# A four-layer graph network on one core: the second layer's own-row work moved into its edge pass, and eight buffers of gathered rows in the third layer's

## The reference

```
out_gnn = relu(xn @ W1.T + segment_sum((xn @ W2.T)[src], dst))
q, k, v = split(xn @ w_qkv + b_qkv)          # 8 heads of 32 columns
k, v    = layernorm(k) * kln_g + kln_b, layernorm(v) * vln_g + vln_b
out     = q @ (k.T @ v / n)                  # per head
ret     = out + xn
h       = gelu(ret @ w1 + b1)
x       = x + out_gnn + (h @ w2 + b2 + xn)
```

## Time and profile before

| | us |
|---|---|
| median of 3 runs (9645.8 to 9689.9) | 9663.9 |
| profiled execution, its own time | 9673.6 |
| its span, first to last instruction | 9671.9 |
| PE busy | 5212.6 (54%) |
| VectorE busy | 5460.1 (56%) |
| ScalarE busy | 1976.8 (20%) |
| GpSimd busy | 3732.0 (39%) |

### The profile page before, as it was taken

How to read it: one execution, slowest core, us unless ns; L and a number is a source line. 1 busy time by engine, 2 the same in 40 slices (tenths; PEclk the granted TensorE clock), 3 DMA queues, 4 the chain that set the end, 5 groups by cost and what they waited for, 6 DMA issues and landing times. The chain is left out here.

```text
span 9671.9 us, 114565 instructions
## 1 busy us (share of the span) xinstructions
PE 5212.6 (54%) x21955; PEld 3844.8 (40%) x21956; DVE 5460.1 (56%) x12451; ACT 1976.8 (20%) x4673; POOL 3732.0 (39%) x3791
## 2 busy tenths in 40 slices
PE   3551454545565545644924454907666676665443
PEld 3551333333344523324813344803444434443243
DVE  5884555656663244464155554144888648885743
ACT  0000333133301100011212211201444124441111
POOL 0884566076501347500136620221655115550003
PEclk9999776767776866676967775958899788887767
DMA  1333333133304623301723311922666136661025
GB/s 56 127 127 41 98 105 99 31 104 101 88 6 140 209 77 88 75 7 59 279 58 84 82 34 51 305 57 90 183 185 186 40 105 183 181 183 47 5 72 168
DMA packets 585603, 1020.35 MB, mean 105 GB/s; under 512 B 187333, under 2 KB 352810, under 8 KB 576714
## 3 DMA queue, kind: packets, MB, share of 16 engines
q0 software_dynamic: 191616, 489.64, 19.4%
q1 hardware_dynamic: 363275, 496.15, 15.6%
q10 hardware_dynamic: 30528, 32.52, 1.0%
HBM read 927.10 MB, written 90.26 MB: 105 GB/s over the span
## 5 line engine op out<-in xcount | busy, mean ns | idle before, releaser
L663 POOL DMA_INDIRECT l_hgt_ep_g<-l_hgt_tkm,l_hgt_ep_ix x832 | 931.5, 1120 | 655.4 <-PE l_hgt_ep_out L739 446.3
L663 POOL DMA_INDIRECT l_gat_ep_g<-l_gat_th,l_gat_ep_ix x832 | 927.5, 1115 | 433.0 <-issue 234.0
L739 PE MATMUL l_hgt_ep_out<-l_hgt_ep_g,l_hgt_ep_here 128*126 128x288 f32 x1664 | 587.9, 508 | 511.4 <-DVE l_hgt_ep_g L874 311.1
L739 PE MATMUL l_gat_ep_out<-l_gat_ep_g,l_gat_ep_here 128*126 128x264 f32 x1664 | 626.5, 536 | 64.0 <-issue 30.0
L739 PEld LDWEIGHTS l_hgt_ep_out<-l_hgt_ep_g,l_hgt_ep_here 128*126 128x126 f32 x1664 | 364.8, 230 | 680.9 <-issue 577.8
L459 POOL DMA_INDIRECT recs<-place_stage,place_pos x400 | 520.4, 1301 | 288.7 <-issue 284.1
L663 POOL DMA_INDIRECT l_ep_g<-l_table,l_ep_ix x416 | 410.8, 987 | 233.6 <-issue 119.7
L1718 POOL IOTA f_moe_route_io<- 1x56 f32 (+2 forms) x4 | 0.7, 166 | 1289.8 <-ACTq L92 1289.8
L1907 DVE TENSOR_TENSOR f_moe_experts_yb<-f_moe_experts_py,f_moe_experts_b2s 128x256 f32<-128x256 f32 x208 | 88.4, 425 | 725.5 <-PE f_moe_experts_py L1890 694.1
L1055 PE MATMUL l_sum_out<-l_sum_g,l_sum_here 128*125 128x256 f32 x832 | 336.7, 540 | 290.4 <-DVE l_g L1080 121.9
L739 PEld LDWEIGHTS l_gat_ep_out<-l_gat_ep_g,l_gat_ep_here 128*126 128x126 f32 x1664 | 414.9, 264 | 188.2 <-issue 61.7
(11 more groups left out here) (575 smaller groups left out, 12169.7 us busy)
## 6 DMA issues: line engine op xcount, KB each, us to landing
l_hgt_ep_hot<-locrow SPq DMA_DIRECT2D x208, 256.0 KB
f_moe_experts_w1b<-in_L_ffn_w SPq DMA_DIRECT2D x32, 1024.0 KB
f_moe_experts_w2b<-in_L_ffn_w SPq DMA_DIRECT2D x32, 1024.0 KB
f_moe_experts_w1b<-in_L_ffn_w SPq DMA_DIRECT2D x64, 512.0 KB
f_moe_experts_w2b<-in_L_ffn_w SPq DMA_DIRECT2D x64, 512.0 KB
f_moe_experts_w1b<-in_L_ffn_W SPq DMA_DIRECT2D x56, 512.0 KB
f_moe_experts_w2b<-in_L_ffn_W SPq DMA_DIRECT2D x56, 512.0 KB
l_gat_ep_hot<-locrow SPq DMA_DIRECT2D x104, 256.0 KB
```

What stands on the lines that cost most here:

```text
L663: gp.indirect_dma_start(g[:, b % 4, j, 0:W], None, table, bass.IndirectOffsetOnAxis(ap=ix[:, b, j:j + 1].bitcast(U32), axis=0)).then_inc(s ...
L739: pe.matmul(out[:, t % 4, 0:WO], here[:, b % 2, t, :], g[:, b, t, F:F + WO], start=True, stop=True).then_inc(s_out, 1)
```

## The change

In the third layer, `edge_pass` of kind "ee" gets NB = 8 buffers of gathered rows, with a semaphore for each, instead of four; the loops of PE, ScalarE and VectorE are unrolled by eight there and GpSimd's by sixteen. The other kinds keep NB = 4.

In the second layer, `edge_sums` is gone and `layer1` is written out. A first phase (l1_pre) transposes each tile of xn once and keeps all 25, multiplies it with W2 and W1 side by side, stores the first as the table (VectorE copies it) and puts the second into the accumulator (ScalarE), in place of the memset. SP loads the weights of the whole layer ahead of the table's stores. VectorE then spreads the gains and takes the mean over each head's 32 columns off the k and v weights and bias, so that k and v come out of the projection with their means removed.

The second phase (l1_edges) is the pass over the edges, written out in straight-line code on PE, ScalarE and VectorE for all 104 chunks, with eight buffers for gathered rows. Between chunks 1 and 46 it projects one of the 25 tiles to k and v every 1.84 chunks, normalises it two and three chunks later, and adds its k.T v four chunks later. Around chunk 50 the mixer's matrix is formed, with the scale on it. From chunk 56 on it makes for each tile the mixer's output and ret, transposed, then the up product with gelu read out of PSUM, then the down product, added to x. x += xn is done per tile. After the last chunk one operation over all rows adds relu of the accumulator to x.

```diff
 def edge_pass(...):
+    NB = 8 if kind == "ee" else 4
-        ix = ph.sb("ix", [128, 8, CT], I32)
-        g = ph.sb("g", [128, 4, CT, max(F + WO, W)])
+        ix = ph.sb("ix", [128, 2 * NB, CT], I32)
+        g = ph.sb("g", [128, NB, CT, max(F + WO, W)])
-                if later(k, 4):
-                    gp.wait_ge(s_out, CT * (k - 3))
+                if later(k, NB):
+                    gp.wait_ge(s_out, CT * (k - NB + 1))
...
-def edge_sums(core, name, acc, table, idx):
...
 def layer1(core, x, xn):
-        edge_sums(core, "l1_sum", g, table, core.e_src)
-            project(core, "l1_self", xn, w, D, ("add", g))
...
+                            for k in range(2):
+                                mm = pe.matmul(out[:, t % 2, h, 0:D], xt[:, t, k, :], wp[:, k, D * h:D * h + D], start=k == 0, stop=k == 1)
...
+            RB = 8
+            SPAN = 46
+            kv_at = {1 + SPAN * t // NT: t for t in range(NT)}
+            out_at = {56 + SPAN * t // NT: t for t in range(NT)}
+            CHAIN = 2 + SPAN * (NT - 1) // NT + 4
...
+                def indices(i, b):
+                    if later(i, RB):
+                        gp.wait_ge(s_out, EG * (i - RB + 1))
+                    gp.tensor_copy(ix[:, b, :], core.e_src[:, bass.ds(i * EG, EG)]).then_inc(s_ix, 1)
...
+            def _(v):
+                edges_here(0)
+                for i in range(NG + 2):
+                    if i + 1 < NG:
+                        edges_here(i + 1)
+                    if 1 <= i <= NG:
+                        add(i - 1)
+                    if i - 1 in kv_at:
+                        t = kv_at[i - 1]
+                        v.wait_ge(s_kv, t + 1)
+                        if t >= 4:
+                            v.wait_ge(s_gram, t - 3)
+                        v.tensor_tensor(y[:, t % 4, :], side[0:P, 0, :], bkv[:, :], ALU.add).then_inc(s_y, 1)
+                        v.tensor_tensor(x[:, t, :], x[:, t, :], xn[:, t, :], ALU.add)
+                    if i - 2 in kv_at:
+                        t = kv_at[i - 2]
+                        v.wait_ge(s_sq, t + 1)
+                        v.tensor_reduce(ve[:, t % 4, :], sq[:, t % 2, :].rearrange("p (h c) -> p h c", c=32), AX.X, ALU.add)
+                        v.drain()
+                        v.tensor_scalar(ve[:, t % 4, :], ve[:, t % 4, :], 1.0 / 32, 1e-5, ALU.mult, ALU.add).then_inc(s_ve, 1)
+                    if i - 3 in kv_at:
+                        t = kv_at[i - 3]
+                        v.wait_ge(s_sd, t + 1)
+                        v.reciprocal(sd[:, t % 4, :], sd[:, t % 4, :])
+                        v.drain()
+                        y3 = y[:, t % 4, :].rearrange("p (h c) -> p h c", c=32)
+                        v.tensor_tensor(y3, y3, sd[:, t % 4, :].unsqueeze(2).to_broadcast([P, 16, 32]), ALU.mult)
+                        v.drain()
+                        v.tensor_tensor(y[:, t % 4, :], y[:, t % 4, :], gain[:, 0, :], ALU.mult)
+                        v.drain()
+                        v.tensor_tensor(y[:, t % 4, :], y[:, t % 4, :], gain[:, 1, :], ALU.add).then_inc(s_ln, 1)
...
+                    if i - 1 in out_at:
+                        t = out_at[i - 1]
+                        v.wait_ge(s_o, t + 1)
+                        if t >= 2:
+                            v.wait_ge(s_up, t - 1)
+                        for r in range(2):
+                            o = v.scalar_tensor_tensor(out=ret[:, t % 2, r, :], in0=side[:, 0, P * r:P * r + P], scalar=cvec[:, r:r + 1], in1=xt[:, t, r, :],
+                                                       op0=ALU.add, op1=ALU.add)
+                        o.then_inc(s_ret, 1)
+                    if i - 4 in out_at:
+                        t = out_at[i - 4]
+                        v.wait_ge(s_down, t + 1)
+                        v.tensor_tensor(x[:, t, :], x[:, t, :], side[0:P, 3, 0:D], ALU.add).then_inc(s_x, 1)
+                v.wait_ge(s_added, TE)
+                v.drain()
+                v.scalar_tensor_tensor(out=x[:, :, :], in0=acc[:, :, :], scalar=0.0, in1=x[:, :, :], op0=ALU.max, op1=ALU.add)
```

More of the change, by code:

```diff
@@ L640, in edge_pass @@
         s_ix, s_parts = ph.sem("ix"), ph.sem("parts")
-        s_g = [ph.sem(f"g{b}") for b in range(4)]
+        s_g = [ph.sem(f"g{b}") for b in range(NB)]
         s_loc = [ph.sem(f"loc{b}") for b in range(2)]
@@ L662, in gather @@
                 for j in range(CT):
[L663 to L665 removed]
+                    gp.indirect_dma_start(g[:, b % NB, j, 0:W], None, table,
+                                          bass.IndirectOffsetOnAxis(ap=ix[:, b, j:j + 1].bitcast(U32), axis=0)).then_inc(s_g[b % NB], 16)
+            piped(gp, NCH, [(0, indices), (1, gather)], 2 * NB)
         @block.sync
@@ L2002, in layer1 @@
     with Phase(core, "l1") as ph:
[L2003 to L2006, removed]
-        edge_sums(core, "l1_sum", g, table, core.e_src)
-        with Phase(core, "l1_v") as pw:
-            w = weights(core, pw, "w", D, ins["L1_gnn_W1T"])
-            project(core, "l1_self", xn, w, D, ("add", g))
-        def relu_add(v):
-            v.scalar_tensor_tensor(out=x[:, :, :], in0=g[:, :, :], scalar=0.0, in1=x[:, :, :], op0=ALU.max, op1=ALU.add)
@@ L2014, in layer1 @@
-        on_vector(core, "l1_relu", relu_add)
-        with Phase(core, "l1_gain") as pg:
-            gain = pg.sb("gain", [P, 2, 512])
-            small = pg.sb("small", [P, 4, 32])
-            move(core, "l1_gains", [(small[:, i, :], ins[f"L1_mix_{n}"].partition_broadcast(P))
-                                    for i, n in enumerate(("kln_g", "vln_g", "kln_b", "vln_b"))])
-            def spread(v):
+        acc = ph.sb("acc", [P, NT, D])
+        xt = ph.sb("xt", [128, NT, 2, P])
+        wkv = ph.sb("wkv", [128, 2, 512])
@@ L2025, in spread @@
                                   small[:, i:i + 1, :].to_broadcast([P, 8, 32]))
-            on_vector(core, "l1_spread", spread)
-            linear_mix(core, "l1_mix", xn, g, "copy", D, 32, 1.0 / N, ins["L1_mix_kv"], ins["L1_mix_WqT"], None,
-                       kv_b=(ins["L1_mix_kv_b"],), q_b=ins["L1_mix_q_b"],
-                       prepare=lambda kv: normalize(core, "l1_kvn", kv, kv, G=16, gain=gain))
-        add_to(core, "l1_ret", g, xn)
-        with Phase(core, "l1_h") as ph2:
-            h = ph2.sb("h", [P, NT, D])
-            w = weights(core, ph2, "w", D, ins["L1_mix_w1"])
-            w2 = weights(core, ph2, "w2", D, ins["L1_mix_w2"])
-            b1 = rowvec(core, ph2, "b1", D, ins["L1_mix_b1"], parts=P)
-            b2 = rowvec(core, ph2, "b2", D, ins["L1_mix_b2"], parts=P)
-            project(core, "l1_up", g, w, D, ("copy", h), bias=b1)
-            on_scalar(core, "l1_gelu", lambda act: act.activation(h[:, :, :], h[:, :, :], ACT.Gelu))
-            project(core, "l1_down", h, w2, D, ("add", x), bias=b2)
@@ L2040, in layer1 @@
-        add_to(core, "l1_bias", x, xn)
+                g3 = wkv[:, :, :].rearrange("p k (h c) -> p (k h) c", c=32)
+                m3 = means[:, :, :, :].rearrange("p k h o -> p (k h) o")
+                b3 = bkv[:, :].rearrange("p (h c) -> p h c", c=32)
+                v.tensor_reduce(m3, g3, AX.X, ALU.add)
+                v.tensor_reduce(bmeans[:, :, :], b3, AX.X, ALU.add)
+                v.drain()
+                v.scalar_tensor_tensor(out=g3, in0=m3.to_broadcast([128, 32, 32]), scalar=-1.0 / 32, in1=g3, op0=ALU.mult, op1=ALU.add)
```

247 lines of the change are left out of this document (236 added, 11 removed).

## The result

The changed kernel takes 9348.2 us (median of 4 runs, 9332.0 to 9371.4) against 9676.9 for the kernel before beside it (4 runs): ratio 0.9662, 95% interval 0.9623 to 0.9702. The forecast of 9375 was 0.3% high.

What follows compares the result with a forecast made beforehand. The second layer's edge pass was taken as near balance: GpSimd's gathers at 5.11 us a chunk, VectorE at 2.9 plus slow spells. Terms -348+28+38-5 = -287 gave 9375 us; own range 9320 to 9430, with rivals 9260 to 9455.

Steps and rivals of the forecast that it cites:

- Own rows, -348: Second layer after the edge pass: the 356.0 us stretch shrinks to one relu-and-add with phase change, 8 us.
- Stage before the pass, +28: Second layer before the edge pass: self product 24, mask phase 1.6, gains and centring 2 us added.
- VectorE's load, 353 us busy: Second layer's edge pass: VectorE's busy time rises from 245 to 353 us with the added own-row work.
- The pass, +38: Second layer's edge pass goes from 622 to 660 us: 672 from VectorE's load, less 12 for eight buffers.
- The line through three passes: Edge-pass time against VectorE's busy time in existing passes: 0.46 us per busy us, giving 672 at 353.
- GpSimd issues at 5.11 a chunk: Second layer's edge pass: GpSimd's pace from index copy to index copy, 531 us for 104 chunks.
- rival A: Second layer's edge pass falls to GpSimd's pace, eight buffers absorbing VectorE's slow spells: pass 550, result 9265; chance 0.14.
- Spells still there, also in straight-line code.: Second layer's edge pass: VectorE's slow spells persist when unrolled, each ending when GpSimd pauses; their absence would show rival A.
- The row against the fetch rule: Second layer's edge pass: rule on branch fetch stalls gives 545 us unrolled; trace row of VectorE instruction counts gives 660.
- B: Second layer's edge pass: PE becomes the bound at half clock, pass 733, result 9448; chance 0.08.
- C: Second layer's edge pass: VectorE idles 0.72 us per instruction, pass 926, result 9641; chance 0.05.
- Third layer, -5: Third layer's edge pass with eight buffers: VectorE stays the bound, change -5 us, bounds -26 and +20.

Runs made afterwards that it cites:

- f1: Changed kernel without the second layer's side work (token mixer and x += xn left out of the edge pass): ratio 0.9717, pass 609.8 us.
- g1: Changed kernel without an edit, run where the kernel before takes 9283.5 us: 9028.9 us, ratio 0.9727.
- f3: Kernel before with nearly only gathers in edge_sums (one product per chunk, one set of masks, no adds): ratio 0.9979, pass 537.5 us.
- e3: Kernel before with PE's and VectorE's edge_sums instructions written out straight-line, four buffers kept: ratio 0.9996, pass 614.5 us.
- e1: Changed kernel with the second layer's index copy back one chunk ahead of its gathers: 9379.3 us, ratio 0.9672.
- e2: Kernel before with the changed kernel's order in edge_sums, index copy right ahead of the gathers needing it: 9696.8 us, ratio 1.0006.
- g3: Changed kernel without index copies in the second layer, GpSimd's code written out, run where the kernel before takes 9283.5: 8962.5 us, ratio 0.9655.
- f2: Changed kernel with four buffers and loops unrolled by four again in the third layer's edge pass: ratio 0.9716.
- h1: Kernel before without an edit, profiled once more: 9728.7 us beside 9684.3.
- e4: Kernel before with eight buffers instead of four in edge_sums, loops kept: ratio 0.9998, pass 626.4 us.

## Why the prediction was right, and where it was not

- **Own rows, -348.** Right: 8.4 us are left, 6.83 of them the one operation over 125x6400.
- **Stage before the pass, +28.** It was 20.3. The price of 24 for a hundred products was nearly right: the hundred before took 27.2, the 200 now 49.1, so 21.9 more. PE's idle time in the stage did not grow (10.6 of 41.5 us before, 9.6 of 61.8 now), so the 3.6 for masks and gains didn't show. The weights and stores queued on SP were hidden, as said, but for 1.6 us in which PE's first product waits for its weights.
- **VectorE's load, 353 us busy.** Right: 357.0.
- **The pass, +38.** Right in sign, wrong in its reason. The line through three passes (0.46 us of pass per us of VectorE) has no cause behind it: f1 and g1 show that all side work, 122 us of VectorE's busy time and 88 of PE's, costs 22 us, and GpSimd's longer issues and copies make up that sum. The first half was to take 6.9 a chunk; 52 chunks took 314.5, 6.05. The step that failed is "GpSimd issues at 5.11 a chunk": the order of copy and gathers in the diff was not compared with the old one, and it makes that 5.68. Had it been, rival A's pass would have been 104x5.68 = 591, and with issues 50 ns longer (1002 against the 952 of f3, 21 us) and the tail of 21, 633.
- **"Spells still there, also in straight-line code."** Wrong for the first half of the pass, though straight-line code indeed doesn't end them (e3, e1): the late copy does, for the edge work (e2). In the second half slow stretches are there, but they don't end in a pause of GpSimd, since the buffers last. Their end at GpSimd's pauses was read rightly, and was the key; the prediction did not ask what pauses the new order makes.
- **The row against the fetch rule.** It was read wrongly. `piped` writes out eight steps, and VectorE's loop begins after the adds of chunk 5, at 3503.8, so half of the first window of the earlier trace rows is loop. What the row was to show is so all the same: chunk 3, in the written-out part, has its four adds spread over 7.4 us, chunk 4 over 2.3. e3 settles it.
- **Rival A** named the right engine and the right sign to look for (no spells, which held for half of the pass), with the wrong price, 550. It is what g3 shows, where there are no spells. **B** did not come: the granted clock rose from 0.67 to 0.80 with the added work, PE busy 447 of 638. **C**: 281 us idle over 800 instructions, 0.35 each instead of 0.72, so idle time was not per instruction.
- **Third layer, -5.** It holds as no effect: 577.6 with four buffers (f2) and 573.4 with eight (g1), and the ratios of the two overlap. On the chip with spells the passes with four took 682.1 to 740.9 (before and h1, with e2 to e4 between), those with eight 691.4 and 712.4 (e1); a size can't be told there.
- **Why the total fitted.** On the chip with spells the pass is held at about 620 us by either limit, as e1 to e4 show: taking one away brings the other. The forecast carried 622 plus a little for the wrong reason. Luck had a part beyond that: the forecast lay 289 us under the time before, measured were 329 between the medians. In the profiles the stages that the diff touches gave 301, and the other 40.6 came where nothing was changed. On the other chip the same change costs an estimated 76 us in the pass (555, worked out, to 631) instead of 17, and -348+76+20 = -252 is left; measured were 9028.9-9283.5 = -254.6, ratio 0.9727.

What stays open: what the spells are, and what differs between the two kinds of chip. e1 and e2 show that they come when GpSimd issues with the copy ahead, and not beside the edge work alone when the copy is late. The changed kernel's second half has slow stretches in spite of the late copy. How much of its 638 us they cost, and whether four buffers would have been enough there, no run shows. Whether it is the chip or a state of it wasn't tried either.

## What to carry to other kernels

Compare the order of the stages on every queue that a diff rewrites: a copy right ahead of its user cost 0.57 us a chunk here, 104 times, and nothing in the instruction counts shows it. Where a stage stands at the same time under four different edits, look for two limits of equal height, and read which one holds from who waits for whom, not from the time. Work hidden under another engine's queue is nearly free (22 us for 122 of VectorE), but fit no slope through other stages: ask what the bounding engine waits for.

## What the runs showed of the hardware

- The same program's passes of gathers take 574 us on one chip and 682 to 741 on another (third layer); as a whole the kernel before takes 9273 to 9284 and 9677 to 9684 (medians). Stages without gathers agree: from the last add of the second layer's pass to the next norm 354.6 us in f3, 356.6 in the kernel before.
- On the slower kind VectorE stands idle for 4 to 10 us before each instruction in such a pass, for some 20 us (e1), and is back at full pace within 6 us after GpSimd stops issuing. A rest of 0.75 us ahead of each four gathers prevents it beside the edge work alone (e2), but not in the changed kernel's second half.
- A gather's issue takes 952 ns alone (f3), 963 beside masks and adds (f1), 1000 beside the full side work (g1).
